# A Mamba and mixture-of-experts layer: decays moved from PSUM to a ring of four in SBUF, PSUM banks shared out anew, two weight matrices streamed

## What is computed

```python
x = x + layernorm(mamba(layernorm(x)))
x = x + layernorm(moe(layernorm(x)))

# mamba, one direction of two (ED = 512 channels, N = 16 states, L = 1024 steps)
x = silu(causal_depthwise_conv(xz_half))          # 4 taps
dbc = x @ Wx.T                                    # delta part 64, B 16, C 16
delta = softplus(delta @ Wdt.T + b_dt)
dA = exp(delta[..., None] * A)                    # A = -exp(A_log)
bx = delta[..., None] * Bm[:, :, None, :] * x[..., None]
h = dAi * h + bxi                                 # step by step over L
y = einsum('ben,bn->be', h, ci) + Dp * x
y = y * silu(z)

# moe: softmax router, top 2 of 8 experts, each 256 -> 512 -> 256 with gelu
```

## Time and profile before

| | us |
|---|---|
| median of 3 runs | 4410.42 |
| lowest and highest | 4407.59, 4414.86 |
| span of the profiled execution, first to last instruction | 4422.2 |

### The profile page before, as it was taken

One profiled execution on the slowest core, in us unless ns is written; L12 is line 12 of the kernel. 1 busy time (PEld: TensorE's weight loads), 2 busy tenths in 40 slices (PEclk: granted clock), 3 DMA queues, 4 the chain that ended last, 5 costly groups with the idle time before them and its releaser, 6 DMA issues.

```text
span 4422.2 us, 57941 instructions
## 1 busy us (share of the span) xinstructions
PE 3604.0 (81%) x18192; PEld 2562.9 (58%) x18192; DVE 3788.5 (86%) x4688; ACT 3101.8 (70%) x5179; POOL 3504.8 (79%) x2085
## 2 busy tenths in 40 slices
PE   4767596888879887798878887798987989788877
PEld 1444454666546655567555774556655665567656
DVE  3999999898998989899898988989999898989710
ACT  4667576787767876688766887678876787668543
POOL 3898887888878888788887888878887888878611
PEclk7878697999979999899879998899998999889988
DMA  6233142556435663357433674345743565336555
GB/s 196 91 107 104 69 150 75 191 183 214 155 104 172 205 210 130 105 182 245 153 124 131 197 238 147 125 151 194 230 141 107 179 220 188 130 113 204 167 167 182
DMA packets 375805, 705.06 MB, mean 159 GB/s; under 512 B 31937, under 2 KB 205514, under 8 KB 371530
## 3 DMA queue, kind: packets, MB, share of 16 engines
q1 hardware_dynamic: 363210, 667.79, 46.0%
q0 software_dynamic: 12288, 33.57, 2.3%
HBM read 529.82 MB, written 171.44 MB: 159 GB/s over the span
## 4 chain that ended last, share of the span: by engine, by line
DVE 29%; PE 25%; POOL 16%; issue 15%; ACT 11%; DMA 3%; SPq 1%; DVEq 0%; POOLq 0%; ACTq 0%
DVE h L1396 10%; POOL drive L1895 9%; DVE h L1393 7%; DVE y L1405 6%; PE h_t L1170 5%; PE side L1204 4%; PE side L1341 4%; PE side L1333 3%; ACT decay L1610 2%; POOL y L1913 2%; POOL xs_dram L1970 2%; DMA expert_w<-in_w 1%; PE side L1318 1%; DVE stats L1450 1%; POOL work L1982 1%
## 5 line engine op out<-in xcount | busy, mean ns | idle before, releaser
L1895 POOL TENSOR_TENSOR drive<-xu,b_row 128x1024 f32<-128x1024 f32 x960 | 2262.7, 2362 | 386.5 <-DVE h L1396 238.8
L1610 ACT ACTIVATE decay<-delta,neg_a 128x512 f32<-128x512 f32 x2048 | 1401.8, 692 | 747.0 <-DVE h L1396 424.5
L1170 PE MATMUL h_t<-ident,h 128*128 128x128 f32 x8192 | 1332.0, 301 | 523.4 <-DVE y L1405 253.4
L1170 PEld LDWEIGHTS h_t<-ident,h 128*128 128x128 f32 x8192 | 1060.1, 155 | 979.1 <-DVE y L1405 373.1
L1405 DVE SCALAR_TENSOR_TENSOR y<-h_t,c_col,y 128x512 f32<-128x512 f32 x1488 | 1085.9, 730 | 54.0 <-PE h_t L1170 52.9
L1913 POOL TENSOR_TENSOR y<-y,scaled 128x512 f32<-128x512 f32 x496 | 631.8, 1274 | 119.4 <-ACT scaled L1631 118.4
L1396 DVE TENSOR_TENSOR_SCAN h<-decay,h,drive 128x512 f32<-128x512 f32 x512 | 654.1, 1278 | 38.6 <-ACT decay L1610 18.6
L1396 DVE TENSOR_TENSOR_SCAN h<-decay,drive 128x512 f32<-128x512 f32 x512 | 622.0, 1215 | 71.9 <-ACT decay L1610 45.8
L1393 DVE TENSOR_TENSOR_SCAN h<-decay,h,drive 128x512 f32<-128x512 f32 x448 | 573.1, 1279 | 44.7 <-ACT decay L1610 23.1
L1393 DVE TENSOR_TENSOR_SCAN h<-decay,drive 128x512 f32<-128x512 f32 x448 | 544.5, 1215 | 76.4 <-POOL drive L1895 55.7
L1204 PE MATMUL side<-prep_work,conv_diag 128*128 128x512 f32 x960 | 460.9, 605 | 27.3 <-DMA prep_work<-xz_dram 19.3
(11 more groups left out here) (205 smaller groups left out, 4355.7 us busy)
## 6 DMA issues: line engine op xcount, KB each, us to landing
expert_w<-in_w SPq DMA_DIRECT2D x350, 512.0 KB, 4.5
b_row<-b_dram SPq DMA_DIRECT2D x240, 512.0 KB, 4.2
x_dram<-xu SPq DMA_DIRECT2D x16, 2048.0 KB, 7.6
delta_dram<-prep_work SPq DMA_DIRECT2D x64, 512.0 KB, 2.9
delta<-delta_dram SPq DMA_DIRECT2D x64, 512.0 KB, 4.9
ys_dram<-work SPq DMA_DIRECT2D x40, 512.0 KB, 6.5
work<-xs_dram SPq DMA_DIRECT2D x38, 512.0 KB, 4.4
h<-in_w SPq DMA_DIRECT2D x34, 512.0 KB, 5.5
```

Source lines behind the costliest of these rows:

```text
L1170: t = pe.e.transpose(h_t[i % N_H_T][:, c * P:(c + 1) * P], its_h[:, c, :], ident[:, :])
L1610: act.e.activation(decay[:, i % N_DECAY, :], delta[:, c, its], ACT.Exp, scale=neg_a[:, c, w % 2, n:n + 1]).then_inc(decay_made, 1)
L1895: op = pool.e.tensor_tensor(drive[:, k % N_DRIVE, :], xu[:, w % 2, c, :], b_row[:, row % N_B_ROW, :], ALU.mult)
```

## The change

- `decay` becomes an SBUF tensor with 4 places of 512 instead of 3 PSUM banks; the scans now find both inputs in SBUF.
- The 8 PSUM banks are 4 for turned tiles (`N_H_T`) and 4 for side pieces (`N_SIDE`).
- The z half of W_in and W_out leave SBUF. They are streamed through `expert_w` as two more loads of 512 KB for each block, kinds "z" and "out" (400 loads instead of 384), and `z_mm` and `out_mm` wait for them.
- `POOL_TILES` names tiles 1, 5, 9, 13 instead of 2, 6, 10, 14. Their number stays.
- `AT` and `BANK_USE` are new tables, with places in 1/256 of a slot.

```diff
-N_DECAY = 3
+N_DECAY = 4
 N_DRIVE = 3
-N_H_T = 3
-N_SIDE = 2
+N_H_T = 4
+N_SIDE = 4
-POOL_TILES = (2, 6, 10, 14)
+POOL_TILES = (1, 5, 9, 13)
-PARTS = 16
+PARTS = 256
+FIRST_EW = (-35807, -35806)
 AT = {
-    "tok_load": [-2240, -2239, 1440, 1696, 5200, 5632, 9168, 9649, 13345, 13824, 17392, 17921, 21632, 22000, 25744,
...
-        "ew_load": ("sp", lambda b: [(i,) for i in range(b * loads + 2, (b + 1) * loads + 2)]),
+        "ew_load": ("sp", lambda b: [(i,) for i in range(b * loads + 2, b * loads + loads + (2 if b < NB - 1 else 0))]),
...
-    ew_order = [("w1", None), ("w2", None)]
-    for blocks in groups:
-        ew_order += [("w1", j) for j in blocks] + [("w2", j) for j in blocks]
-    loads = len(ew_order)
+    ew_order = []
+    for b in range(NB):
+        ew_order += [(b, kind, None) for kind in ("z", "out") if b < NB - 1] + [(b, "w1", None), (b, "w2", None)]
+        if b == NB - 2:
+            ew_order.append((NB - 1, "z", None))
+        for blocks in groups:
+            ew_order += [(b, "w1", j) for j in blocks] + [(b, "w2", j) for j in blocks]
+        if b == NB - 2:
+            ew_order.insert(-2, (NB - 1, "out", None))
+    loads = len(ew_order) // NB
...
-        w_in_sb = sb("w_in_sb", [P, DC, 2 * ED])
+        w_in_sb = sb("w_in_sb", [P, DC, ED])
-        w_out_sb = sb("w_out_sb", [P, EC, D])
+        decay = sb("decay", [P, N_DECAY, BANK])
-        decay = ctx.enter_context(nc.psum_tensor("decay", [P, N_DECAY, BANK], F32))
...
                 elif piece == "z_mm":
+                    wz = weights_in(pe, b, "z", None).rearrange("p (c n) -> p c n", n=ED)
                     for k in range(DC):
-                        mm = pe.e.matmul(bank[:, :], w_in_sb[:, k, ED + c * P:ED + (c + 1) * P],
+                        mm = pe.e.matmul(bank[:, :], wz[:, k, c * P:(c + 1) * P],
...
                 elif piece == "out_mm":
-                    pe.wait_ge(const_in["w_out"], 16)
+                    wo = weights_in(pe, b, "out", None).rearrange("p (c n) -> p c n", n=D)
...
                 elif piece == "ew_load":
+                        if its_kind == "z":
+                            sp.wait_ge(done["z_mm"], nth("z_mm", pb, NH - 1, EC - 1))
+                        elif its_kind == "out":
+                            sp.wait_ge(done["out_mm"], nth("out_mm", pb, TB - 1))
```

More of the change, by code:

```diff
@@ new lines @@
+    "d_make": [-35837],
+    "cw_store": [-35826, -35818, -35811, -35803, -35800, -35793, -35790, -35787],
+    "proj": [1540, 1541, 1542, 1543, 1544, 1545, 1546, 1547, 30208, 30209, 32257, 32768, 34560, 34816, 36352,
[4 rows of a table added]
+    "d_store": [-35825],
+    "xz_copy": [-35831, -35829, -35827, -35825, -35823, -35821, -35820, -35816, 30464, 30720, 32768, 33024,
[5 rows of a table added]
+    "tap": [-250, -249, -248, -247, -246, -245, -244, -243],
+    "d_load": [-35817, -35550, -35387, -35230, -35075, -34915, -34759, -34722],
+    "xn_store": [-35824, -35764, -35648, -35516, -35354, -35197, -35046, -34889],
@@ new lines @@
+    "u_mul": [-35835, -1024, -511, 1, 18432, 19968, 21504, 23040, 43520, 44544, 46080, 47616, 79872, 80896,
[4 rows of a table added]
+    "delta_store": [-35815, -35810, -35802, -35799, -35776, -35774, -35772, -35771, -35742, -35740, -35738,
[5 rows of a table added]
+    "ew_load": [-35805, -35694, -35675, -35674, -35671, -35666, -35665, -35660, -35659, -35657, -35656, -35654,
[30 rows of a table added]
+    "delta_load": [-35812, -35804, -35801, -35797, -35763, -35762, -35760, -35758, -35727, -35726, -35725,
[5 rows of a table added]
+    "xz_load": [-35798, -35795, -35791, -35789, -35737, -35722, -35713, -35704, -35607, -35573, -35557, -35554,
+        -35448, -35422, -35405, -35400, -35286, -35268, -35248, -35243, -35131, -35110, -35090, -35082, -34974,
+        -34952, -34939, -34928, -34818, -34796, -34776, -34768],
@@ L752, in mamba_moe @@
     plan.put("sp", next(places["xn_load"]), "xn_load", NB - 1)
[L753 to L754 removed]
+    plan.put("sp", B1_AT, "b1_load")
+    plan.put("sp", ZERO_AT, "zero_store")
     plan.close()
@@ L850, in mamba_moe @@
         wide = [wide[:, i, :] for i in range(2 * EC * L // (DC * H))]
-        ALL_WIDE = (NB - 1) * loads + 2
+        ALL_WIDE = ew_at[NB - 1, "w2", None] + 1
         first_xz = h[:, :, :, :].rearrange("p k c t -> p (k c t)")[:, 0:EC * XZW].rearrange("p (c t) -> p c t", c=EC)
@@ L1104, in weights_in @@
         def weights_in(pe, b, kind, j):
-            i = b * loads + ew_at[kind, j]
+            i = ew_at[b, kind, j]
             place, which_load = ew_place(i)
@@ new lines, in transfer @@
+                    b, kind, j = ew_order[i]
+                    if i < 3:
+                        sp.wait_ge(drive_made, 1)
+                    if ew_before(i) is None:
+                        sp.wait_ge(turned, NW * TILES)
+                    elif ew_before(i) >= 0:
+                        pb, its_kind, its_j = ew_order[ew_before(i)]
+                        if its_kind == "z":
+                            sp.wait_ge(done["z_mm"], nth("z_mm", pb, NH - 1, EC - 1))
+                        elif its_kind == "out":
+                            sp.wait_ge(done["out_mm"], nth("out_mm", pb, TB - 1))
+                        elif its_j is None and its_kind == "w1":
+                            sp.wait_ge(done["h1_mm"], nth("h1_mm", pb, NH - 1, HC - 1))
+                        elif its_j is None:
+                            sp.wait_ge(done["eo_mm"], nth("eo_mm", pb, NH - 1, QB - 1))
+                        elif its_kind == "w1":
+                            sp.wait_ge(done["r1_mm"], nth("r1_mm", pb, its_j, 1))
+                        else:
+                            sp.wait_ge(done["r2_mm"], nth("r2_mm", pb, its_j))
@@ new lines, in transfer @@
+                    if kind == "z":
+                        src = w_in_t[:, ED:2 * ED]
+                    elif kind == "out":
+                        src = w_out_t
+                    elif j is None:
+                        src = (w1 if kind == "w1" else w2)[NX - 1]
+                    else:
+                        sp.wait_ge(done["slots"], nth("slots", b))
+                        expert = sp.e.value_load(owner_i[0:1, j:j + 1], min_val=0, max_val=E - 1)
+                        src = (w1 if kind == "w1" else w2)[bass.ds(expert, 1), :, :].rearrange("a k n -> (a k) n")
```

336 lines of the change are left out of this document (147 added, 189 removed), and 661 rows, old and new, of tables (AT, BANK_USE).

## The result

The changed kernel takes 5881.57 us (median of 4, 5876.94 to 5889.20), the kernel before 4412.64 us on the same chip. The ratio is 1.3332, with a 95% interval of 1.3313 to 1.3350: 33% slower. The forecast was 6060 us.

The account below looks back on a forecast made before the run. No engine alone bounded the kernel, DVE being nearest. Turns 5413 + uncovered sums 272 + other DVE work 45 + before the scans 77 + behind 265 = 6072 us profiled, the median 12 us below: 6060 us, range 5450 to 6600.

Parts of the forecast that it names:

- The scans are held by POOL, and POOL by the scans: DVE scans with both inputs in SBUF and POOL operations reading SBUF take turns: 5746.5 us by full durations.
- Rival 2: Only DVE waits; POOL's adds and `u_mul` go on half under scans, 390 us less: about 5700 us; chance 0.12.
- Two signs of the prediction: In the profile after, scans have a mean well above 2 us and end just behind an operation of POOL.
- The turns, 5413 us: Scans and POOL's SBUF-reading operations in turn: 5746.5 us of full durations, less 333 us passing under waits.
- the lower bound that I gave, 5100 us: Turns of scans and POOL if only the streaming parts exclude each other: 2193 + 2367 + 540 us.
- What can't lie under a turn, 317 us: DVE work with no POOL turn beside it: a quarter of the sums, 272 us, and 45 us of other work.
- Before and behind the scans, 342 us: Time before the first scan, 77 us, and behind the last, 265 us, left as they are; tail possibly shorter.
- Rings and banks cost nothing and give nothing: Ring of four decays, four tile banks, four side banks: the waits they target vanish under DVE's waits for POOL; gain nothing.
- ACT, 68 us more, hidden: ACT writing 2048 decays to SBUF at 33 ns more each adds 68 us, hidden under its waits for scans.
- Streamed weights: Sixteen more loads of 512 KB through `expert_w` cost nothing, at most 20 us for each of 8 blocks.
- Rival 1: Scans run beside POOL unheld and the deeper rings gain: 4280 us (4240 to 4400); chance 0.08.
- Rival 3: Nothing lies under POOL's turns, so most of DVE's 1238 us comes on top: 6650 us or more; chance 0.05.

Follow-up runs that it names:

- e2: The changed kernel with POOL's drive replaced by three memsets, so the drive writes SBUF and reads nothing: 4766.8 us, ratio 1.0794.
- e1: The kernel before with its decay ring of three in SBUF, x half of W_in used for the z half and W_out: 6266.9 us, ratio 1.4187.
- e5: The kernel of e1 with POOL's tiles 1, 5, 9, 13 in place of 2, 6, 10, 14: 5929.5 us, ratio 1.3428 to the kernel before.
- e6: The kernel of e1 with a ring of four decays instead of three: 6270.4 us, ratio 1.4188 to the kernel before.
- e9: The kernel before with four decays, first halves' in PSUM, second halves' in SBUF, x half of W_in as in e1: 5017.1 us, ratio 1.1356.
- e4: The kernel before with no tiles for POOL but the first state's, so DVE has 496 more sums: 4561.4 us, ratio 1.0327.
- e7: The kernel before, decays in PSUM, with POOL's tiles 1, 5, 9, 13: 4476.5 us, ratio 1.0130.
- e8: The kernel before with five tiles of sixteen for POOL (2, 5, 8, 11, 14): 4482.5 us, ratio 1.0149.
- e11: The kernel before with three tiles of sixteen for POOL (2, 8, 14): 4502.7 us, ratio 1.0202.
- e12: The kernel before with POOL's tiles 0, 4, 8, 12: 4570.5 us, ratio 1.0358.

## Why the prediction was right

*The scans are held by POOL, and POOL by the scans.* Right, both ways. That POOL waits no row of before showed; now the adds take 2060 ns and the drives 2996. The Trainium skill's rule ("SBUF — State Buffer", "Who interferes with whom") agrees: both sides wait, and e2 shows that a POOL operation that only writes holds nothing. That the hold lasts for the whole instruction, as that page of the skill also says (section "SBUF: two separate sides"), the runs don't bear out: a saturated round is 9.73 us, while the full durations of its seven operations add up to some 11.0. Rival 2 (only DVE waits) falls with the same rows. Two signs of the prediction were off. The scans' mean is 2.05 us, not well above 2. And a held scan ends 1.09 us behind POOL's operation, not just behind it as the small router operations did, since its whole stream comes after.

*The turns, 5413 us.* The step that was mis-sized. I took 333 us off the full durations, for what passes under a wait. In the steady stretch only the streaming part excludes, 9.72 us of 9.73, so the lower bound that I gave, 5100 us, is the price of the turns, and 313 us less than my term.

*What can't lie under a turn, 317 us.* Also mis-sized, to the other side. The scans' stretch is 5583 us, so 483 us of it aren't turns. In the steady stretch it is none at all: a round has three sums and three turns of POOL, and each sum lies beside one. Most of it lies where router, norms and POOL's indirect transfers stand (30 scans in 100 us instead of 41). The sum had no term for POOL's other work, 3504.8 - 3196.4 = 308 us before and 4727.2 - 4291.0 = 436 us now, most of it these issues; by the estimate above 156 us of the loss lie in them. No run took router, norms or issues away, so the split isn't shown. That a quarter of the sums would stand alone was an average over a pattern which I hadn't drawn: e1 and e5 show that one slot of difference in POOL's tiles changes the time by 337 us.

*Before and behind the scans, 342 us.* It was 64 + 241 = 305: the tail shortened by 24 us, which I had named as possible. Together 5100 + 483 + 305 = 5888, the profiled span. Against my terms that is 313 us less, 166 more and 37 less, 184 us less than 6072 in all. That the total is off by less than the turns alone is luck: the two large errors have opposite signs.

*Rings and banks cost nothing and give nothing.* Right for the ring (e6). All of the change but the placement and the odd tiles gives 48 us together (e5 against the changed kernel); the banks weren't tried by themselves.

*ACT, 68 us more, hidden.* 59 us more (1461.1 against 1401.8), hidden.

*Streamed weights.* Not tried by themselves; only the 48 us of gain, in which a cost of theirs may hide, are known.

*Rival 1 (the scan isn't held).* False. *Rival 3 (nothing lies under POOL's turns).* Not reached; e1, with another order, came to 6267 of its 6650 us.

## What to carry to other kernels

Before moving a DVE operand from PSUM to SBUF, look at what GpSimd does at that time. Here every sum, with one input in SBUF and one in PSUM, ran beside GpSimd at 0.72 us, while scans with two SBUF inputs took turns with the GpSimd operations that read SBUF, and the streaming times of both added up. A few tiny router operations in the old trace, 0.23 us alone and up to 2.3 beside POOL, were enough to see it. Where such turns can't be avoided, count the gaps between them, and see that each operation which needs no turn lies beside one of the other engine: here that was worth 337 us, and a deeper ring nothing. Count too what the other engine does besides its turns: while it issues transfers it feeds nobody.

## What the runs showed of the hardware that was not expected

- The fixed part of an operation, about 0.14 us of a scan and 0.19 of a drive (what is left of 1215 and 2362 ns beside their streaming), isn't under the exclusion: in a saturated stretch the round is the streaming sum to 0.01 us.
- Turns don't always alternate. The scan at 1792.94 above takes 6.78 us: it starts 0.16 us behind the start of a drive, and is kept out by that drive, an add and another drive, which ends at 1798.63; the scan ends 1.09 us later. In the steady stretch a waiting scan got in between two operations of POOL each time. In the changed kernel 28 of 2048 scans take over 3.6 us; 12 of them start 0.14 to 0.16 us behind the start of a POOL operation with more directly behind it, and 12 others while POOL issues an indirect transfer. What decides wasn't settled.
- One DVE operation with a single SBUF input is held as well: a tensor-scalar on 8 elements, which takes 0.17 us beside an idle POOL. The old trace had it too (4 of 8, up to 2.03 us), and it isn't among the 17 cases of the prediction, which have two inputs. DVE, then POOL:

```profile
1765.31 2.25 DVE L1592 TENSOR_SCALAR ends<-steps_of 128x8 f32<-128x8 f32 x1
```

```profile
1765.17 2.35 POOL L1945 TENSOR_TENSOR drive<-xu,b_row 128x1024 f32<-128x1024 f32 x1 [2.99 <-DVE h L1446]
```

- POOL's issues of indirect transfers got longer too, 1398 and 1217 ns in the mean against 989 and 963 before. It goes with the placement: e1 has 1525 and 1329, e9 1287 and 1194, and the runs with decays in PSUM (e4, e7, e8, e11, e12) 985 to 988 and 961 to 964. That they read their indices through the same port would fit, and wasn't tried.

```profile
L2020 POOL DMA_INDIRECT xs_dram<-work,slot_i x112 | 156.6, 1398 | 74.2 <-DVE owner_hot L1611 37.9 <-issue 35.6 <-POOL y L1963 0.7
L2032 POOL DMA_INDIRECT work<-ys_dram,slot_i x128 | 155.8, 1217 | 139.6 <-DMA ys_dram<-work 102.6 <-issue 33.3 <-PE side L1368 3.0
```
